# Group norm and a column convolution: Pool's sums of means ahead of its last addition, newton and the other small steps one place later

## The reference

```python
# x: (32, 384, 56, 56) f32; weight (384, 1, 56, 1); bias (384,)
def _gn(v, G=32, eps=1e-5):
    B_, C_, H_, W_ = v.shape
    g = v.reshape(B_, G, C_ // G, H_, W_)
    m = jnp.mean(g, axis=(2, 3, 4), keepdims=True)
    s = jnp.var(g, axis=(2, 3, 4), keepdims=True)
    return ((g - m) / jnp.sqrt(s + eps)).reshape(v.shape)

y = _gn(x)
y_cat = jnp.concatenate([y, y[:, :, :-1, :]], axis=2)      # wraps around in H
out = conv_general_dilated(y_cat, weight, (1, 1), 'VALID', feature_group_count=384)
return x + out + bias[None, :, None, None]
```

## Time and profile before

| | |
|---|---|
| median of 3 runs | 877.93 us (875.45 to 880.6) |
| the profiled execution, its own time | 881.76 us |
| its span | 879.9 us |
| mean granted TensorE clock | 0.925 of full speed |
| busy: PE, DVE, ACT, Pool | 83%, 77%, 75%, 65% |
| DMA | 340.64 MB, mean 387 GB/s |

### The profile page before, as it was taken

One profiled execution on the slowest core, in us unless ns is written; L12 is line 12 of the kernel. 1 busy time (PEld: TensorE's weight loads), 2 busy tenths in 40 slices (PEclk: granted clock), 3 DMA queues, 4 the chain that ended last, 5 costly groups with the idle time before them and its releaser, 6 DMA issues.

```text
span 879.9 us, 8182 instructions
## 1 busy us (share of the span) xinstructions
PE 732.7 (83%) x1920; PEld 513.0 (58%) x1920; DVE 679.5 (77%) x1538; ACT 662.8 (75%) x1026; POOL 571.2 (65%) x1102
## 2 busy tenths in 40 slices
PE   0688898889889888878788887988878988889895
PEld 0456666666566666556565564665655656566664
DVE  7888878897787878778777677877877887788842
ACT  1788788788788878778677776787877867778784
POOL 2467767676676666666675656676766667567665
PEclk9999979998898999899898899899989989899998
DMA  9999999999999999999999999999999999999986
GB/s 355 410 387 399 383 407 396 406 413 410 403 394 374 377 391 389 405 392 388 401 381 396 370 361 386 398 403 398 403 389 387 392 402 400 390 401 409 405 306 229
DMA packets 39472, 340.64 MB, mean 387 GB/s; under 512 B 5008, under 2 KB 5120, under 8 KB 8704
## 3 DMA queue, kind: packets, MB, share of 16 engines
q1 hardware_dynamic: 39424, 340.13, 99.1%
HBM read 185.97 MB, written 154.14 MB: 387 GB/s over the span
## 4 chain that ended last, share of the span: by engine, by line
DMA 52%; PE 13%; POOL 13%; ACT 10%; DVE 8%; issue 3%; SPq 0%; POOLq 0%; ACTq 0%
DMA out<-xt 28%; DMA xt<-x 24%; PE conv L402 12%; POOL xt L235 10%; ACT xn L330 7%; DVE st L264 5%; ACT xn L338 3%; DVE xt L281 2%; PE p_mean L378 1%; POOL newt L227 1%; POOL rstd L228 1%; POOL newt L226 1%; POOL newt L225 1%; POOL shift L229 0%; PE p_var L387 0%
## 5 line engine op out<-in xcount | busy, mean ns | idle before, releaser
L402 PE MATMUL conv<-xn,runs 112*112 112x448 f32 x1536 | 694.5, 602 | 24.6 <-DMA runs<-taps 10.9
L330 ACT ACTIVATE xn<-xt,shift,rstd 112x672 f32<-112x672 f32 x512 | 463.1, 942 | 140.1 <-POOL xt L235 140.1
L402 PEld LDWEIGHTS conv<-xn,runs 112*112 112x112 f32 x1536 | 465.6, 314 | 167.3 <-issue 64.7
L264 DVE BATCH_NORM_STATS2 st<-xt 112x6 f32<-112x336 f32 x1024 | 451.4, 494 | 109.5 <-DMA xt<-x 109.3
L235 POOL TENSOR_TENSOR xt<-xt,xn 112x448 f32<-112x448 f32 x384 | 431.2, 1136 | 81.0 <-ACT xn L338 80.8
L281 DVE SCALAR_TENSOR_TENSOR xt<-conv,bias_all,xt 112x448 f32<-112x448 f32 x384 | 258.5, 673 | 81.1 <-PE conv L402 80.5
L338 ACT ACTIVATE xn<-conv,bias_all 112x448 f32<-112x448 f32 x384 | 235.7, 626 | 47.7 <-PE conv L402 44.9
L378 PE MATMUL p_mean<-msum,neg_mean 112*112 112x8 f32 x128 | 24.5, 263 | 112.2 <-POOL msum L204 112.2
L214 POOL TENSOR_TENSOR dev<-st,nmean 112x16 f32<-112x16 f32 x128 | 24.9, 216 | 134.6 <-ACT nmean L314 134.6
L378 PEld LDWEIGHTS p_mean<-msum,neg_mean 112*112 112x112 f32 x128 | 19.3, 191 | 150.2 <-POOL msum L204 134.4
L386 PEld LDWEIGHTS p_var<-st,avg 112*112 112x112 f32 x128 | 23.6, 210 | 40.6 <-POOL dev L218 25.9
(11 more groups left out here) (23 smaller groups left out, 69.4 us busy)
## 6 DMA issues: line engine op xcount, KB each, us to landing
xt<-x SPq DMA_DIRECT2D x128, 1344.0 KB, 10.6
out<-xt SPq DMA_DIRECT2D x128, 1176.0 KB, 12.9
runs<-taps SPq DMA_DIRECT2D x64, 147.0 KB
bias_all<-bias SPq DMA_DIRECT2D x1, 168.0 KB, 14.1
```

The source lines that it names most:

```text
L264: ins = nc.vector.bn_stats(st[:, n % RS, h, b, :], xt[0:P, n % XS, h, b * ROW:(b + 1) * ROW])
L330: ins = nc.scalar.activation(xn[:, n % NS, :, part], xt[0:P, n % XS, :, part], ACT.Identity, scale=rstd[:, n % RS, b:b + 1], bias=shift[:, ...
L402: nc.tensor.matmul(bank(c), lay[:, :, c], channel_of(xn, u % NS, c), start=True, stop=True).then_inc(conv_ready, 1)
```

## The change

No instruction is added or taken away. On Pool, the sums of means (add_means) of a unit are made one pass earlier, ahead of the last addition; the deviations stand behind the first addition instead of ahead of it; newton stands behind the fourth addition (channel 7) instead of behind the third. On ACT, root goes behind the eviction of channel 7. On DVE, add_vars and invert stand one output step later. On PE, the matmul of the means goes behind channel 2's convolution (was 1), those of the variance behind channel 5's (was 4).

```diff
@@ -238,18 +238,21 @@
                 add_means(n)
                 deviations(n)
                 newton(n)
+            add_means(LEAD_COEF)
 
             for u in range(UNITS):
                 n = u + LEAD_COEF
-                if n < UNITS:
-                    add_means(n)
+                add_x(u, ACT_CH[0])
+                if n < UNITS:
                     deviations(n)
-                for c in ACT_CH[:3]:
+                for c in ACT_CH[1:4]:
                     add_x(u, c)
                 if n < UNITS:
                     newton(n)
-                for c in ACT_CH[3:]:
-                    add_x(u, c)
+                add_x(u, ACT_CH[4])
+                if n + 1 < UNITS:
+                    add_means(n + 1)
+                add_x(u, ACT_CH[5])
 
         @block.vector
         def _(dve):
@@ -302,9 +305,9 @@
                         stats(u + LEAD_STATS, ends[k - 1] if k else 0, ends[k])
                     take(u, c)
                     if u + LEAD_COEF < UNITS:
-                        if k == 2:
+                        if k == 3:
                             add_vars(u + LEAD_COEF)
-                        if k == 3:
+                        if k == 4:
                             invert(u + LEAD_COEF)
 
         @block.scalar
@@ -361,11 +364,11 @@
                 if n < UNITS:
                     normalize(n, 4, 5)
                 evict(u, ACT_CH[2])
+                if n < UNITS:
+                    normalize(n, 5, 7)
+                evict(u, ACT_CH[3])
                 if m < UNITS:
                     root(m)
-                if n < UNITS:
-                    normalize(n, 5, 7)
-                evict(u, ACT_CH[3])
                 if n < UNITS:
                     normalize(n, 7, BP)
                 for c in ACT_CH[4:]:
@@ -412,9 +415,9 @@
                 for c in range(CG):
                     convolve(u, c)
                     if n < UNITS:
-                        if c == 1:
+                        if c == 2:
                             mean(n)
-                        if c == 4:
+                        if c == 5:
                             variance(n)
 
 
```

More of the change, by code:

```diff
@@ L363, in _ @@
                 evict(u, ACT_CH[2])
-                if m < UNITS:
-                    root(m)
                 if n < UNITS:
@@ L368, in _ @@
                 evict(u, ACT_CH[3])
+                if m < UNITS:
+                    root(m)
                 if n < UNITS:
```

## The result

The changed kernel takes 933.43 us (median of 4 runs, 932.85 to 936.57) against 876.69 us before on the same chip: ratio 1.063, 95% interval 1.059 to 1.068. It is slower, as forecast, by 57 us (forecast: 930, range 906 to 960). The profiled execution has a span of 932.0 us. Medians are over all runs and ratios over the fast ones alone (some runs of one and the same kernel take over 1.5% longer than its fastest), so the two need not agree to the last digit.

A forecast was written before the change was run, and what follows sets the result against it. DMA at 13.3 us per unit was taken to bound the kernel, the engines' 12.23 lying below. Changed: 13.86 + 0.2 = 14.06; 60 such cycles from 47.0, a last of 13.56, tail 26.6, less some 3: 930 us, range 906 to 960.

The forecast's parts named there:

- The chain of a unit: Path through ACT and Pool between successive units' first normalizations: 13.86 us instead of 12.23, so +1.63 per unit.
- Newton's place: On Pool behind channel 7's addition, newton no longer lies under the wait for that channel's eviction: about 1.1 us per unit.
- The sums ahead of the last addition: Sums of means on Pool, moved ahead of channel 11's addition, now delay the next normalization: 0.50 us per unit.
- The deviations at nothing: Deviations on Pool behind channel 1's addition end before channel 3's eviction is through: 0 on this path.
- PE's moves at nothing: Mean behind channel 2, variance behind channel 5: PE's gain isn't on the path, as ACT waits for Pool.
- The clock: Low PE clock after stands delays convolutions that ACT wants: 0.2 us per unit taken, between bounds of 0 and 0.97.
- Rival A: PE's longer stand before the variance lowers the clock in every unit: 977 us, 955 to 1000; chance 0.14.
- The transfers stop being the bound: DMA's 13.3 us per unit lies under 14.06; late loads vanish, DMA below 97% and near 366 GB/s.
- B: Rival: the DMA hides the change, the cycle staying under 13.44 us: 882 us, within the noise; chance 0.07.
- C: Rival: PE's stand before the mean goes, later units run at 12.78 instead of 13.44 us: 854 us; chance 0.05.
- D: Rival: half of the delay, since loads and Pool interlock otherwise than thought: 895 to 910 us; chance 0.08.
- The ends: Outside the cycles: second unit's T at 47.0, tail unchanged at 26.6 us, some 3 us subtracted for the median.

The follow-up runs named there:

- e14: Changed kernel with two extra 448-column matmuls per unit on PE ahead of the variance, adding nothing to the result: 917.52 us, ratio 1.039.
- e12: Changed kernel with sums of means and deviations back at the head of the pass, newton being Pool's only move: 904.79 us, ratio 1.028.
- e3: Kernel before with one edit, the next unit's sums of means ahead of channel 11's addition on Pool: 882.3 us, ratio 1.003.
- e4: Changed kernel with PE's matmuls at their old places (mean behind channel 1, variance behind channel 4): 981.26 us, ratio 1.118.
- e1: Changed kernel with newton, root, add_vars and invert at their old places and PE's variance back behind channel 4: 953.81 us, ratio 1.087.
- e7: Changed kernel with newton, root, add_vars and invert at their old places, PE's variance staying behind channel 5: 906.59 us, ratio 1.041.
- e9: Kernel before with one edit, the deviations on Pool behind channel 1's addition: 887.19 us, ratio 1.011.
- e11: Changed kernel with two extra small Pool multiplications per unit between the sums of means and channel 11's addition: 988.28 us, ratio 1.120.
- e2: Kernel before with one edit, newton on Pool behind channel 7's addition: 1015.01 us, ratio 1.157.
- e8: Kernel before with PE's two edits alone (mean behind channel 2, variance behind channel 5): 882.2 us, ratio 0.998.
- e10: e8 with loads of only the 112 used rows instead of 128: 925.93 us, ratio 1.053.
- e13: e7 with one extra 448-column matmul per unit on PE ahead of the variance, adding nothing to the result: 883.7 us, ratio 1.008.

## Why the prediction was right, step by step

- **The chain of a unit.** Right: 13.86 worked out, 13.80 in the trace, 13.77 on average without low clock (e14).
- **Newton's place.** Right: undisturbed units go from 12.23 to 13.31 with newton as Pool's only move (e12), 1.08 where "about 1.1" stood. The 1.06 us that Pool stands before channel 7, where the prediction had about 1, is that step seen in the profile.
- **The sums ahead of the last addition.** Right in size: 0.46 in the row, and 13.31 to 13.80 from e12 to the change. Where the transfers pace (e3) the same move costs nothing that can be measured.
- **The deviations at nothing, PE's moves at nothing.** Only their sum was right. Of PE's new order the prediction wrote "What it gains isn't on the path". With PE's order of before, the same Pool order takes 48 us more (e4), and e1 without the later variance 47 us more than e7. In the order before, the deviations' move alone costs 0.52 us per unit (e9). The later deviations would delay channel 5's convolution, and PE's edit is what takes them out of its way. Each was priced with the other in place and the condition not said.
- **The clock, 0.2 us per unit.** Right in size (0.26), and the mechanism is seen: the stand before the variance is followed by the 1.2 GHz level. But 0.2 was picked between bounds of 0 and 0.97, so that it came so near is partly luck. The stand is 2.0 us in the unit shown and 2.1 on average, not 2.7. Nor is the cycle a constant 13.9 to 14.3: half of the units lose nothing and seven lose over 1 us, about the upper bound. Rival A was right in that nearly every unit is touched (mean clock 0.888, channels 9 and 11 late), wrong in that it decides: Pool's newton covers them. ACT's wait for Pool is 1.9 us, not 3.5, since part of it has become waiting for PE. How near A was is seen in e11, where over a third of the loss came with a lower clock, and in e2, where by the traces it was more than the edit's own cost.
- **The transfers stop being the bound.** Right: 109.3 us of DVE's waits become 4.8, 96.5% and 365 GB/s where "below 97% and near 366" stood. That they were the bound before is shown by e8 (faster units, same time) and e10 (slower transfers, more time); rivals B and C fall with that and with e14, and D, half of the delay, with the time itself.
- **The ends.** The second unit's T came at 47.77 (forecast 47.0), the tail was 28.3 us (26.6): 2.4 us too little, half of it set off by the 61 units (855.9 us, forecast 857.2). The 3 us taken off for the median weren't there; own time 933.8 and median 933.4 agree.

Not settled: what exactly makes the clock fall in one unit and not in the next. In the kernel before, the stand of 1.54 us at 148.57 is followed by six matmuls in 2.62 us, at full clock; the one ahead of the slower unit is as long, and six matmuls behind it take 4.32 us:

```profile
160.80 0.36 PE L378 MATMUL p_mean<-msum,neg_mean 112*112 112x8 f32 x2 [1.53 <-POOL msum L204]
```

e13 and e14 show only that filling the stand keeps the clock up.

None of these versions beats the kernel before: e3, e8 and e13 are at its time within 1%, paced by the same transfers.

## What to carry to other kernels

Write out the chain of one undisturbed round as a sum of rows and see that it gives the round's length; only then move steps, and ask of each whether it leaves a wait that covered it. A step moved later on one engine and the consumer's step moved later on another are one edit: price each without the other too, since the pair may be free and either half cost 5%. Where two engines' chain and the transfers lie close together (14.03 and 13.3 us here), the DMA share needn't tell which rules; what the issuing queue waits for did.

## What was not expected of the hardware

- Loads onto 112 partitions instead of 128, of the same row length, ran at 268 instead of 401 GB/s while loads ran alone, and at 360 instead of 400 with loads and stores mixed (e10 against e8), so 318.62 MB took longer than 340.64. Why was not tried.
- Useless matmuls made a kernel faster by 16 us (e14, 933.4 to 917.5) and 23 us (e13, 906.6 to 883.7), and the granted clock rose from 0.888 to 0.997 and from 0.884 to 0.959 with them.
- A delay of 0.5 us per unit on Pool (e11) cost 0.9 us on average, and the mean granted clock of PE fell from 0.888 to 0.853 with it. Here one engine's order went with another engine's speed.
